# Finer waits at the down-projections, the MLP and the FFN, and the last residual adds of an out-projection ahead of a low half

## The chip, the cores and the metric

One core of one Trainium2 chip (trn2). The metric is the device time of one execution in microseconds; the number given for a kernel is the median of its runs.

## The reference

One decoder layer with pre-norms on x of shape (4, 512, 512): four batches of 512 positions with 512 features. Three sublayers follow each other, each on the layer norm of x and each added to x.

```python
x = x + _L0_attn_ref(_layernorm(x), ...)      # Mamba block, then an MLP
x = x + _L0_xattn_ref(_layernorm(x), w1, w2)  # int8 linear, silu gate, int8 linear
x = x + _L0_ffn_ref(_layernorm(x), ...)       # 4-bit weights, gelu gate
...
h = res + _mamba(_rmsnorm(hidden_states, rms1_w), ...)   # ends with y @ out_proj_w.T
hn = _rmsnorm(h, rms2_w)
mlp = silu(hn @ gate_w.T) * (hn @ up_w.T) @ down_w.T     # 2048 inner features
return h + mlp
...
inter = gelu(xt @ Wg.T) * (xt @ Wu.T)                    # 4096 inner features
out = inter @ Wd.T
```

Everything is fp32 at the interface.

## The kernel before, in words

The activations lie with features on the 128 partitions: `res` holds 4 feature tiles (f) of 4 x 512 positions. A product in nearly full fp32 is done in three passes: both operands are split into a high half (fp32r) and a low half (the rest), and `three_pass` (L1729) issues high x high (L1733), high x low (L1734) and low x high (L1735) into one PSUM bank. Weights are `ghi`/`glo`, the normed inputs of batch b are `xh[b]`/`xl[b]`, the inner activations `ahi`/`alo`. ACT makes high halves (a copy into fp32r), DVE low halves (a subtraction).

There are two phases. Phase 1 (to about 1065 us) is the Mamba scan; the change doesn't touch it. Phase 2 has these stages, written as one instruction stream per engine, tied by semaphores; nothing but the program order and the waits sets the order on an engine.

**Out-projection.** 16 chunks m, four per batch (c = m % 4), each 2 of 8 inner tiles. DVE multiplies y by silu(z) (`gate_u`, L1437), ACT makes the high half, DVE the low half (`u_low`, L1442), PE does 24 matmuls into banks 0 to 3, one per feature tile f (`out_project`, L1852). After the last chunk of a batch, `add_out` (L1448) adds the four banks to `res`, one DVE add each (L1452); it counts `outp_added`. Beside it the RMS norm of batches 0 and 1 is done: squares on ACT (L985), sums on POOL (L1217, L1220), a mean matmul (L1868), root on ACT, `rms_scale` on DVE (L1468, 4 instructions), high half on ACT (L992, counts `r_hi`), low half on DVE by `split_low` (L1475, one instruction over 128x2048, writes `xl`, counts `r_lo`). In DVE's loop over m (L1478) `split_low` of batch 0 stands at m = 13 and of batch 1 at m = 17; `add_out` of batches 1 to 3 stands at m = 9, 13 and 17, behind `rms_scale` and `split_low` of the same m. POOL adds the layer's input to `res` (`add_input`, L1209).

**MLP and FFN.** PE's loop over blocks p (L2004) has 24 groups E of 24 blocks i. The groups go through MLP half h = 0 (E 0 to 3, batches 0 and 1), MLP h = 1 (E 4 to 7, batches 2 and 3), FFN h = 0 (E 8 to 15) and FFN h = 1 (E 16 to 23). A group makes 4 inner tiles j for its two batches and projects them down:

- i = 0 to 15: gate and up products in turn, 12 matmuls each. n = i // 2 numbers the 8 pairs: tile j = n // 2, batch n % 2. Block 0 and 1 so read the first batch of the half, block 2 and 3 the second.
- ACT applies silu or gelu to the gate bank (L1094), DVE multiplies by the up bank (L1677, counts `prod_done`), ACT makes `ahi` (L1099), DVE `alo` (L1684, counts `a_lo`, in the order n = 0, 1, ... 7).
- i = 16 to 23: the down-projection, four blocks (f = 0 to 3) for the first batch, four for the second, 12 matmuls each: three per inner tile j. DVE adds each bank to `res` (`add_down`, L1663).

Blocks take banks in turn, p % 5; `bank_taken` (L1992) waits until the bank's last reader is through. Weights come by DMA into two tiles; FFN weights are unpacked on DVE (L1506 to L1510), scaled on POOL (L1231), then split (L965 on ACT, L1459 on DVE) into a ring of 5; PE waits for `w_lo`.

The waits that the change is about, at L2007 to L2010 and L2027: at the first group of each half PE waits for both batches' `xl`; block 0 waits for all 16 out-projection adds; and the first block of each batch's down-projection waits for the `alo` of that batch's last tile:

```python
if i == 0 and q == 0:
    pe.wait_ge(n_lo if ffn else r_lo, 2 * h + 2)
if p == 0:
    pe.wait_ge(outp_added, FT * B)
...
if f == 0:
    pe.wait_ge(a_lo, 8 * E + 7 + bb)
```

The second sublayer ("attention" in the code) and the norm of the third run as background steps between the blocks (`background`, L415): transposes and products on PE, and on DVE, ACT and POOL reductions, clips, scalings and norm steps, each placed at a fixed block number in each engine's loop. The norm steps' low half is again `split_low`, with `n_hi` and `n_lo`.

Of the kernel before, what the change touches and what calls it, by code (L numbers as in the profile page):

```python
# [24 lines left out]
P = 128  # L25
B, S, D = 4, 512, 512
T = B * S
FT = D // P
# [18 lines left out]
OCH = 4  # L47
# [9 lines left out]
WRING = 5  # L57
# [5 lines left out]
def build(nc, t, out):  # L63
# [79 lines left out]
    def post(name, shape, dt, at):  # L143
        return place(name, shape, dt, at)

    R1 = FREE0
    ghi = [post(f"ghi{s}", [P, 1024], F32R, R1 + 8192 * s) for s in range(WRING)]
    glo = [post(f"glo{s}", [P, 1024], F32R, R1 + 8192 * s + 4096) for s in range(WRING)]
    ahi = [post(f"ahi{j}", [P, 2 * S], F32R, R1 + 40960 + 8192 * j) for j in range(4)]
    alo = [post(f"alo{j}", [P, 2 * S], F32R, R1 + 40960 + 8192 * j + 4096) for j in range(4)]  # L150
# [61 lines left out]
    with ctx:  # L212
        def sem(name):
            return ctx.enter_context(nc.semaphore(name))
# [83 lines left out]
        outp_added = sem("outp_added")  # L298
# [7 lines left out]
        r_lo = sem("r_lo")  # L306
# [14 lines left out]
        a_lo = sem("a_lo")  # L321
        down_ready = sem("down_ready")
# [10 lines left out]
        n_lo = sem("n_lo")  # L333
# [12 lines left out]
        def cols(b, n=S):  # L346
            return slice(b * n, (b + 1) * n)
# [44 lines left out]
        def stage(Q):  # L392

            if Q < MLP_Q:
                return False, Q // MLP_PAIRS, Q % MLP_PAIRS
            return True, (Q - MLP_Q) // FFN_PAIRS, (Q - MLP_Q) % FFN_PAIRS
# [11 lines left out]
        def free_bank(V):  # L408
            return V % 5
# [14 lines left out]
        def x_step(r):  # L424
            return r - 2 if r >= 5 else r - 1 if r in (1, 2, 3) else -1

        def n_step(r):
            return r - 1 if r != 4 else -1
# [845 lines left out]
        def _(dve):  # L1274
# [47 lines left out]
            def w_low(n):  # L1322
                dve.wait_ge(whi_ready, n + 1)
                dve.tensor_tensor(wlo[n % 3][:, :, :], wraw[:, n % 2, :, :],
                                  whi[n % 3][:, :, :].bitcast(F32), ALU.subtract)\
                   .then_inc(wlo_ready, 1)
# [110 lines left out]
            def gate_u(m):  # L1437
                dve.wait_ge(sz_ready, m + 1)
                dve.tensor_tensor(uraw[m % CHUNKS][:, :, :], uraw[m % CHUNKS][:, :, :],
                                  zraw[m % CHUNKS][:, :, :], ALU.mult).then_inc(u_ready, 1)  # L1440

            def u_low(m):  # L1442
                dve.wait_ge(uhi_ready, m + 1)
                dve.tensor_tensor(ulo[m % CHUNKS][:, :, :], uraw[m % CHUNKS][:, :, :],
                                  uhi[m % CHUNKS][:, :, :].bitcast(F32), ALU.subtract)\
                   .then_inc(ulo_ready, 1)

            def add_out(b):  # L1448
                dve.wait_ge(res_loaded[b], 16)
                for f in range(FT):  # L1450
                    dve.wait_ge(outp_ready, FT * b + f + 1)
                    dve.tensor_tensor(res[:, f, cols(b)], res[:, f, cols(b)], ps[:, f, :], ALU.add)\  # L1452
                       .then_inc(outp_added, 1)
# [11 lines left out]
            def rms_scale(b):  # L1465
                dve.wait_ge(r_rooted, b + 1)
                for f in range(FT):
                    last = dve.scalar_tensor_tensor(  # L1468
                        out=xlr[b][:, f, :], in0=res[:, f, cols(b)], scalar=rms2[:, f:f + 1],
                        in1=rs_r[b % 2][:, :], op0=ALU.mult, op1=ALU.mult)  # L1470
                last.then_inc(r_scaled, 1)

            def split_low(b, hi_done, lo_done):
                dve.wait_ge(hi_done, b + 1)
                dve.tensor_tensor(xl[b][:, :, :], xlr[b][:, :, :], xh[b][:, :, :].bitcast(F32),  # L1475
                                  ALU.subtract).then_inc(lo_done, 1)

            for m in range(OCH * B + 2):  # L1478
                if m < OCH * B:
                    gate_u(m)  # L1480
                if 1 <= m <= OCH * B:
                    u_low(m - 1)
                if m in (5, 6, 11):
                    w_low((5, 6, 11).index(m))
                for b in range(2):
                    if m == OCH * b + 12:
                        rms_scale(b)
                    if m == OCH * b + 13:
                        split_low(b, r_hi, r_lo)
                if m % OCH == 1 and m > OCH:  # L1490
                    add_out(m // OCH - 1)

            link = linked(e["chain"])

# [171 lines left out]
            for p in range(24 * ALL_E + 1):  # L1666
                E, i = divmod(p, 24)
# [39 lines left out]
        def _(pe):  # L1707
# [21 lines left out]
            def three_pass(out_, pairs_, start=True, stop=True):  # L1729

                n = len(pairs_)
                for k, (w_h, w_l, x_h, x_l) in enumerate(pairs_):
                    pe.matmul(out_, w_h, x_h, start=(start and k == 0), stop=False)  # L1733
                    pe.matmul(out_, w_h, x_l, start=False, stop=False)  # L1734
                    last = pe.matmul(out_, w_l, x_h, start=False, stop=(stop and k == n - 1))  # L1735
                return last
# [115 lines left out]
            def out_project(m, f):  # L1852

                c = m % OCH
                w = slice(f * P, (f + 1) * P)
                s = m % CHUNKS
                return three_pass(ps[:, f, :], [(owhi[:, OCT * c + k, w], owlo[:, OCT * c + k, w],
                                                 uhi[s][:, k, :], ulo[s][:, k, :]) for k in range(OCT)],
                                  start=(c == 0), stop=(c == OCH - 1))
# [11 lines left out]
            def rms_var(b):  # L1871
                pe.wait_ge(r_summed, b + 1)
                bg_bank(b)
                mean(b, xhr[b])

            for m in range(OCH * B):
# [3 lines left out]
                for f in range(FT):  # L1880
                    if m >= OCH and m % OCH == 0:
                        pe.wait_ge(outp_added, FT * (m // OCH - 1) + f + 1)
                    last = out_project(m, f)
# [108 lines left out]
            def bank_taken(V):  # L1992

                if V >= 5:
                    E, i = divmod(V - 5, 24)
                    if i >= 16:
                        pe.wait_ge(added, 8 * E + i - 15)
                    elif i % 2:
                        pe.wait_ge(prod_done, 8 * E + i // 2 + 1)
                    else:  # L2000
                        pe.wait_ge(act_done, 8 * E + i // 2 + 1)
                return ps[:, free_bank(V), :]

            for p in range(24 * ALL_E):  # L2004
                E, i = divmod(p, 24)
                ffn, h, q = stage(2 * E)
                if i == 0 and q == 0:  # L2007
                    pe.wait_ge(n_lo if ffn else r_lo, 2 * h + 2)
                if p == 0:
                    pe.wait_ge(outp_added, FT * B)  # L2010
                if i < 16:
                    n, w = divmod(i, 2)
                    j, b = n // 2, 2 * h + n % 2
                    T = 6 * E + 2 * (n // 4) + w
                    at = P * (j % 2)
                    if n % 4 == 0:
                        pe.wait_ge(w_lo, T + 1)
                    three_pass(bank_taken(p), [
                        (ghi[T % WRING][:, 256 * f + at:256 * f + at + P],
                         glo[T % WRING][:, 256 * f + at:256 * f + at + P],  # L2020
                         xh[b][:, f, :], xl[b][:, f, :]) for f in range(FT)])\
                        .then_inc(up_ready if w else gate_ready, 1)
                else:
                    bb, f = divmod(i - 16, 4)
                    if i == 16:
                        pe.wait_ge(w_lo, 6 * E + 6)
                    if f == 0:  # L2027
                        pe.wait_ge(a_lo, 8 * E + 7 + bb)
                    d = [((6 * E + 4 + j // 2) % WRING, D * (j % 2) + P * f) for j in range(4)]
                    three_pass(bank_taken(p), [  # L2030
                        (ghi[s][:, at:at + P], glo[s][:, at:at + P],
                         ahi[j][:, cols(bb)], alo[j][:, cols(bb)]) for j, (s, at) in enumerate(d)])\
                        .then_inc(down_ready, 1)
                for b in (2, 3):
                    if p == 12 * (b - 2) + 3:
                        rms_var(b)
                for h_, r in background(p):
                    for bb in range(2):
                        attend(2 * h_ + bb, x_step(r - X_LEN * bb))
                    for bb in range(2):  # L2040
                        norm_step(2 * h_ + bb, n_step(r - 2 * X_LEN - 2 - bb))
# [79 lines left out]
```

## Time and profile before

| | |
|---|---|
| median of 3 runs | 2873.14 us (2871.67 to 2876.65) |
| profiled execution, its own time | 2876.27 us |
| its span | 2874.5 us |
| mean granted clock of the matrix engine | 0.944 |
| busy: PE, DVE, ACT, POOL | 2651.7 us (92%), 2129.6 (74%), 1152.1 (40%), 1255.9 (44%) |
| chain that ended last | PE 71%, DVE 11%, ACT 9%, issue 5% |

A profiled execution lists each instruction with its start and length. PE is the matrix engine, PEld its weight loads, DVE the vector engine, ACT the scalar engine, POOL GpSimd. PE's lengths overlap: a 512-column matmul is shown with 0.39 us, and the next one starts 0.23 us after it, so the distance between starts is what counts. In square brackets stands the idle time before an instruction and what released it; "issue" means that the profile found no releaser. Clocks are shares of the full 2.4 GHz.

### The profile page before, as it was taken

The page shows a single profiled execution, that of the slowest core. Times are in us where ns is not written, and L with a number is a line of the kernel's source. Part 1 is how long each engine was busy: PE and PEld are TensorE (multiplying, and loading weights), DVE is VectorE, ACT ScalarE, POOL GpSimd, SP SyncE. Part 2 cuts the span into 40 slices and gives each one's busy share as a digit, 9 for nine tenths or more (in the row PEclk, how much of TensorE's full clock was granted, in tenths as well). Part 3 has the DMA queues.
Part 4 walks back from the last instruction along what each step waited for, and adds up shares of the span by engine and source line. Part 5 has one row for each costly group of instructions (what it writes and reads, how often), then busy time and mean ns, then how long its engine had stood idle before and what let it go on. Part 6 is the DMA issues. An engine that isn't in the chain of part 4 may idle for free.

```text
span 2874.5 us, 32445 instructions
## 1 busy us (share of the span) xinstructions
PE 2651.7 (92%) x11096; PEld 1880.8 (65%) x11096; DVE 2129.6 (74%) x2731; ACT 1152.1 (40%) x1690; POOL 1255.9 (44%) x836
## 2 busy tenths in 40 slices
PE   7888888888899878999999999999989999999999
PEld 3443444444344326788887777887877788888887
DVE  4999999999999985543366677777767865555563
ACT  4555555555555534432244443443333322222221
POOL 2789888888889871110010023222212522222220
PEclk8998998989889769999999999999999999999999
DMA  6654654554465436221111112112111111111111
GB/s 230 209 157 121 188 157 121 157 166 129 132 183 154 133 99 231 81 76 49 52 66 59 45 37 67 44 45 67 44 37 45 44 49 48 51 45 52 50 47 66
DMA packets 152310, 275.35 MB, mean 96 GB/s; under 512 B 27345, under 2 KB 27857, under 8 KB 151633
## 3 DMA queue, kind: packets, MB, share of 16 engines
q1 hardware_dynamic: 152144, 273.27, 31.5%
q8 instruction: 88, 1.44, 0.2%
q14 instruction: 78, 0.63, 0.1%
HBM read 178.01 MB, written 61.34 MB: 83 GB/s over the span
## 4 chain that ended last, share of the span: by engine, by line
PE 71%; DVE 11%; ACT 9%; issue 5%; POOL 2%; DMA 1%; SPq 1%; DVEq 0%; POOLq 0%; ACTq 0%
PE ps L1733 19%; PE ps L1734 18%; PE ps L1735 18%; PE ps L1772 8%; DVE state L1358 6%; ACT ps L847 5%; PE ps L1784 4%; POOL read L1172 1%; DMA uraw<-y_d 1%; PE ps L1924 1%; PE ps L1868 1%; PE ps L1898 1%; DVE drive L1349 1%; DVE act_o L1677 0%; POOL xhr L1217 0%
## 5 line engine op out<-in xcount | busy, mean ns | idle before, releaser
L1172 POOL TENSOR_TENSOR read<-state,c_t 128x512 f32<-128x512 f32 x512 | 664.0, 1308 | 138.2 <-DVE state L1358 118.5
L1358 DVE TENSOR_TENSOR_SCAN state<-ps,drive 128x512 f32<-128x512 f32 x512 | 622.3, 1216 | 14.3 <-ACT ps L847 12.8
L1733 PE MATMUL ps<-xh,ghi 128*128 128x512 f32 x1536 | 609.1, 397 | 5.7 <-issue 5.7
L1231 POOL TENSOR_TENSOR wdeq<-packed,scales 128x1024 f32<-128x1024 f16 x96 | 260.2, 2711 | 798.3 <-DVE packed L1510 798.3
L1735 PE MATMUL ps<-xh,glo 128*128 128x512 f32 x1536 | 599.3, 390 | 0.0
L1734 PE MATMUL ps<-xl,ghi 128*128 128x512 f32 x1536 | 599.2, 390 | 0.0
L847 ACT ACTIVATE ps<-ps,a_exp 128x512 f32<-128x512 f32 x512 | 338.9, 662 | 473.8 <-PE ps L1772 472.5
L1772 PE MATMUL ps<-dpack,sel 128*128 128x512 f32 x512 | 260.9, 510 | 114.2 <-DVE state L1358 112.1
L1677 DVE TENSOR_TENSOR act_o<-act_o,ps 128x512 f32<-128x512 f32 x192 | 131.7, 686 | 313.4 <-PE ps L1735 298.5
L1349 DVE TENSOR_TENSOR drive<-ps,b_t 128x512 f32<-128x512 f32 x512 | 344.1, 672 | 12.7 <-PE ps L1772 11.9
L1099 ACT ACTIVATE ahi<-act_o 128x512 fp32r<-128x512 f32 x192 | 121.4, 632 | 562.6 <-DVE act_o L1677 562.6
L1733 PEld LDWEIGHTS ps<-xh,ghi 128*128 128x128 f32 x1536 | 289.4, 188 | 68.7 <-issue 9.2
L1734 PEld LDWEIGHTS ps<-xl,ghi 128*128 128x128 f32 x1536 | 289.4, 188 | 62.1 <-issue 3.1
L1735 PEld LDWEIGHTS ps<-xh,glo 128*128 128x128 f32 x1536 | 289.1, 188 | 60.7
L1733 PE MATMUL ps<-ahi,ghi 128*128 128x512 f32 x768 | 306.3, 399 | 20.2 <-issue 20.2
L1735 PE MATMUL ps<-ahi,glo 128*128 128x512 f32 x768 | 300.6, 391 | 0.0
L1734 PE MATMUL ps<-alo,ghi 128*128 128x512 f32 x768 | 300.6, 391 | 0.0
L1772 PE MATMUL ps<-vpack,sel 128*128 128x512 f32 x512 | 251.3, 491 | 28.6 <-DVE drive L1349 16.7
L1663 DVE TENSOR_TENSOR res<-res,ps 128x512 f32<-128x512 f32 x192 | 130.9, 685 | 192.6 <-PE ps L1735 190.0
L1772 PEld LDWEIGHTS ps<-dpack,sel 128*128 128x128 f32 x512 | 107.8, 211 | 244.1 <-DVE state L1358 235.3
L1772 PEld LDWEIGHTS ps<-vpack,sel 128*128 128x128 f32 x512 | 105.8, 207 | 225.2 <-DVE drive L1349 115.3
L965 ACT ACTIVATE ghi<-wdeq 128x1024 fp32r<-128x1024 f32 x96 | 100.9, 1051 | 297.7 <-POOL wdeq L1231 266.0
(204 smaller groups left out, 3775.3 us busy)
## 6 DMA issues: line engine op xcount, KB each, us to landing
whi<-w_d SPq DMA_DIRECT2D x63, 256.0 KB, 4.1
wlo<-w_d SPq DMA_DIRECT2D x63, 256.0 KB, 4.6
dpack<-dh SPq DMA_DIRECT2D x64, 128.0 KB, 3.8
dpack<-dl SPq DMA_DIRECT2D x64, 128.0 KB, 3.6
b_d<-ev SPq DMA_DIRECT2D x32, 256.0 KB
x_d<-ev SPq DMA_DIRECT2D x32, 256.0 KB, 2.6
vpack<-vh SPq DMA_DIRECT2D x64, 128.0 KB, 3.5
vpack<-vl SPq DMA_DIRECT2D x64, 128.0 KB, 2.8
```

The lines of the kernel that those rows point to most:

```text
L847: act.activation(ps[:, n % 2, :], ps[:, n % 2, :], ACT.Exp, scale=a_exp[:, col:col + 1]).then_inc(decay_ready, 1)
L1099: act.activation(ahi[n // 2][:, cols(n % 2)], act_o[n % 2][:, :], ACT.Copy)\
L1172: pool.tensor_tensor(read[:, n % RRING, :], state[:, n % SRING, :], c_t[:, g % 2, :], ALU.mult).then_inc(read_ready, 1)
L1231: pool.tensor_tensor(wdeq[:, :].rearrange("p (h n) -> p h n", h=2), codes, scale, ALU.mult).then_inc(deq, 1)
L1349: dve.tensor_tensor(drive[:, n % DRING, :], ps[:, 2 + n % 2, :], b_t[:, g % 2, :], ALU.mult).then_inc(drive_ready, 1)
L1358: dve.tensor_tensor_scan(state[:, n % SRING, :], ps[:, n % 2, :], drive[:, n % DRING, :], 0.0, ALU.mult, ALU.add)\
L1663: dve.tensor_tensor(res[:, f, cols(b)], res[:, f, cols(b)], ps[:, free_bank(24 * E + 16 + k), :], ALU.add).then_inc(added, 1)
L1677: dve.tensor_tensor(act_o[n % 2][:, :], act_o[n % 2][:, :], ps[:, free_bank(24 * E + 2 * n + 1), :], ALU.mult)\
L1733: pe.matmul(out_, w_h, x_h, start=(start and k == 0), stop=False)
L1734: pe.matmul(out_, w_h, x_l, start=False, stop=False)
L1735: last = pe.matmul(out_, w_l, x_h, start=False, stop=(stop and k == n - 1))
L1772: pe.matmul(ps[:, bank, :], sel[:, 4 * (j % 2) + m, :], pack[j // 2][:, :], start=True, stop=True).then_inc(done, 1)
```

## The change

In DVE's loop of the out-projection `add_out` moves ahead of `rms_scale` and `split_low` of the same m, which matters at m = 13 (adds of batch 2, low half of batch 0) and m = 17 (adds of batch 3, low half of batch 1). At the first group of a half, block 0 waits for the first batch's low half only, and block 2 for the second's. Blocks 0 to 3 wait for one add of batch 3 each, instead of block 0 for all. In a down-projection's first block of each batch, PE waits ahead of each inner tile j for that tile's `alo`; the matmuls and their order stay the same.

```diff
--- before.py
+++ after.py
@@ -1482,13 +1482,13 @@
                     u_low(m - 1)
                 if m in (5, 6, 11):
                     w_low((5, 6, 11).index(m))
+                if m % OCH == 1 and m > OCH:
+                    add_out(m // OCH - 1)
                 for b in range(2):
                     if m == OCH * b + 12:
                         rms_scale(b)
                     if m == OCH * b + 13:
                         split_low(b, r_hi, r_lo)
-                if m % OCH == 1 and m > OCH:
-                    add_out(m // OCH - 1)
 
             link = linked(e["chain"])
 
@@ -2004,10 +2004,10 @@
             for p in range(24 * ALL_E):
                 E, i = divmod(p, 24)
                 ffn, h, q = stage(2 * E)
-                if i == 0 and q == 0:
-                    pe.wait_ge(n_lo if ffn else r_lo, 2 * h + 2)
-                if p == 0:
-                    pe.wait_ge(outp_added, FT * B)
+                if q == 0 and i in (0, 2):
+                    pe.wait_ge(n_lo if ffn else r_lo, 2 * h + 1 + i // 2)
+                if p < FT:
+                    pe.wait_ge(outp_added, FT * (B - 1) + p + 1)
                 if i < 16:
                     n, w = divmod(i, 2)
                     j, b = n // 2, 2 * h + n % 2
@@ -2024,13 +2024,15 @@
                     bb, f = divmod(i - 16, 4)
                     if i == 16:
                         pe.wait_ge(w_lo, 6 * E + 6)
-                    if f == 0:
-                        pe.wait_ge(a_lo, 8 * E + 7 + bb)
-                    d = [((6 * E + 4 + j // 2) % WRING, D * (j % 2) + P * f) for j in range(4)]
-                    three_pass(bank_taken(p), [
-                        (ghi[s][:, at:at + P], glo[s][:, at:at + P],
-                         ahi[j][:, cols(bb)], alo[j][:, cols(bb)]) for j, (s, at) in enumerate(d)])\
-                        .then_inc(down_ready, 1)
+                    bank = bank_taken(p)
+                    for j in range(4):
+                        s, at = (6 * E + 4 + j // 2) % WRING, D * (j % 2) + P * f
+                        if f == 0:
+                            pe.wait_ge(a_lo, 8 * E + 2 * j + bb + 1)
+                        last = three_pass(bank, [(ghi[s][:, at:at + P], glo[s][:, at:at + P],
+                                                  ahi[j][:, cols(bb)], alo[j][:, cols(bb)])],
+                                          start=(j == 0), stop=(j == 3))
+                    last.then_inc(down_ready, 1)
                 for b in (2, 3):
                     if p == 12 * (b - 2) + 3:
                         rms_var(b)
```

## Rows read from the trace of the kernel before

**Rows 1.** windows: length, busy PE PEld DVE ACT POOL, granted clock, DMA share, GB/s

```profile
1183.00:2874.00 1691.00, 1657.99 (x7492) 1353.29 (x7492) 1062.24 (x1491) 547.97 (x744) 343.29 (x133) 0.99 0.16 51
```

**Rows 2.** waits of PE from 1176 us on: total us, times, longest

```profile
PE ps L1733 <- issue: 25.9, 7, 7.8
```

**Rows 3.** PE groups by form from 1183 us on: busy, mean ns, idle before

```profile
L1733 PE MATMUL ps<-xh,ghi 128*128 128x512 f32 x1536 | 609.1, 397 | 5.7 <-issue 5.7
...
L1733 PE MATMUL ps<-ahi,ghi 128*128 128x512 f32 x768 | 306.3, 399 | 20.2 <-issue 20.2
```

**Rows 4.** PE timeline: start us, length us, instruction, idle before

```profile
1160.74 0.39 PE L1733 MATMUL ps<-uhi,owhi 128*128 128x512 f32 x1
...
1176.84 0.39 PE L1735 MATMUL ps<-uhi,owlo 128*128 128x512 f32 x1
1182.88 0.77 PE L1733 MATMUL ps<-xh,ghi 128*128 128x512 f32 x1 [5.66 <-issue]
...
1186.22 0.40 PE L1735 MATMUL ps<-xh,glo 128*128 128x512 f32 x1
```

**Rows 5.** DVE timeline, end of the out-projection

```profile
1149.49 2.28 DVE L1475 TENSOR_TENSOR xl<-xlr,xh 128x2048 fp32r<-128x2048 f32 x1
...
1155.50 0.69 DVE L1452 TENSOR_TENSOR res<-res,ps 128x512 f32<-128x512 f32 x1 [0.68 <-PE ps L1735]
...
1157.24 1.22 DVE L1444 TENSOR_TENSOR ulo<-uraw,uhi 128x1024 fp32r<-128x1024 f32 x1
...
1170.83 2.73 DVE L1468 SCALAR_TENSOR_TENSOR xlr<-res,rms,rs_r 128x512 f32<-128x512 f32 x4
1175.54 4.85 DVE L1475 TENSOR_TENSOR xl<-xlr,xh 128x2048 fp32r<-128x2048 f32 x1 [1.99 <-ACT xh L992]
1180.31 2.47 DVE L1452 TENSOR_TENSOR res<-res,ps 128x512 f32<-128x512 f32 x4
```

**Rows 6.** PE timeline, first matmuls of six down-projections

```profile
1739.17 0.77 PE L1733 MATMUL ps<-ahi,ghi 128*128 128x512 f32 x1 [6.16 <-issue]
...
1954.84 0.47 PE L1733 MATMUL ps<-ahi,ghi 128*128 128x512 f32 x1 [2.41 <-issue]
...
2026.52 0.47 PE L1733 MATMUL ps<-ahi,ghi 128*128 128x512 f32 x1 [0.51 <-issue]
...
2104.44 0.77 PE L1733 MATMUL ps<-ahi,ghi 128*128 128x512 f32 x1 [7.78 <-issue]
...
2182.57 0.67 PE L1733 MATMUL ps<-ahi,ghi 128*128 128x512 f32 x1 [2.12 <-issue]
...
2186.29 0.39 PE L1733 MATMUL ps<-ahi,ghi 128*128 128x512 f32 x1
...
2257.62 0.47 PE L1733 MATMUL ps<-ahi,ghi 128*128 128x512 f32 x1 [1.23 <-issue]
```

**Rows 7.** DVE timeline ahead of the matmul at 2104.44

```profile
2089.82 0.68 DVE L1684 TENSOR_TENSOR alo<-act_o,ahi 128x512 fp32r<-128x512 f32 x1
...
2103.66 0.68 DVE L1684 TENSOR_TENSOR alo<-act_o,ahi 128x512 fp32r<-128x512 f32 x1
```

**Rows 8.** POOL timeline, same stretch

```profile
1173.63 4.61 POOL L1209 TENSOR_TENSOR res<-res,xraw 128x2048 f32<-128x2048 f32 x1 [3.81 <-DVE xlr L1468]
1179.31 3.29 POOL L1217 TENSOR_TENSOR xhr<-xhr 128x1024 f32<-128x1024 f32 x1 [1.07 <-ACT xhr L985]
```

**Rows 9.** windows, columns as in rows 1, after two of those waits

```profile
1954.00:1958.00 4.00, 3.17 (x18) 2.50 (x19) 3.36 (x7) 1.58 (x2) 0.00 (x0) 1.00 0.42 125
2182.00:2187.00 5.00, 4.43 (x13) 3.52 (x14) 2.96 (x5) 3.54 (x6) 0.00 (x0) 0.66 0.32 102
```

**Rows 10.** waits of DVE from 1183 us on

```profile
DVE act_o L1677 <- PE ps L1735: 298.5, 144, 5.1
```

**Rows 11.** PEld and PE timelines at a block's start

```profile
1729.91 0.19 PEld L1733 LDWEIGHTS ps<-xh,ghi 128*128 128x128 f32 x1
...
1730.13 0.39 PE L1733 MATMUL ps<-xh,ghi 128*128 128x512 f32 x1
```

## The prediction

> **What bounds the kernel now.** I read the windows first. From 1183 us to the end the matrix engine (PE) is busy 1658 of 1691 us, DVE 1062 [rows 1]. So the MLP and FFN go at PE's pace, and only what stands between its matmuls can be won. Of PE's waits from 1176 us on, one row is large: 25.9 us in 7 waits, put down to "issue", that is, to nothing the profile names [rows 2]. Grouped by form, 5.7 us of it stands before the first gate/up matmul and 20.2 us before matmuls that read ahi, the down-projections [rows 3]. The pace is 24 matmuls per 5.44 us: 71 steps from 1160.74 to 1176.84 give 0.2268 us each [rows 4].
>
> The first wait: out-projection's last matmul starts at 1176.84, the MLP's first at 1182.88 [rows 4]. What released it is on DVE: rms scale of batch 1 ends at 1173.6, xl of batch 1 (split_low) runs 1175.54 to 1180.39, the four last residual adds 1180.31 to 1182.78 [rows 5], 0.1 us before PE starts. The wait at block 0 asks for all of that, although block 0 reads batch 0 and bank 0 only.
>
> The six others stand before the first matmul of a down-projection [rows 6]; the other 18 have none. The largest ends at 2104.44; DVE ended the alo of its fourth intermediate tile at 2104.34, that of its third at 2090.50 [rows 7]. The wait is for a_lo; PE had the first three tiles' inputs 6 us before it stopped.
>
> **Part 1, start of the MLP.** Block 0 now asks for r_lo 1 (batch 0, whose split started at 1149.49 [rows 5]) and outp_added 13. The adds of batch 3 move ahead of split_low(1). Four adds cost 0.62 us each (2.47 for 4); the first three can go while PE works on the next bank, the fourth when PE is through at about 1177.2. The out-projection's chunk 15 takes 5.44 us from 1171.6, so bank 0 is full at about 1173.2, and DVE is free of rms_scale at 1173.6 [rows 5]. So add 13 is done near 1174.3 and block 0 follows the out-projection without a gap. Gained are the 6.04 us between starts less one step of 0.23: 5.81 us.
>
> Also the slow clock. After that wait 8 steps (1182.88 to 1186.22) take 3.34 us instead of 8 x 0.2268 = 1.81 [rows 4]: 1.53 us more. Without the wait this goes.
>
> What is late next: split_low(1), read by block 2 at 1177.07 + 24 x 0.2268 = 1182.5. DVE reaches it at 1178.0. With POOL at rest such a split takes 2.28 us (1149.49); beside POOL's add of 1173.63 to 1178.24 it took 4.85, ending 2.15 after POOL [rows 5, 8]. So the likely end is about 1180.4, as now: cost 0. If instead POOL's pair sum (now at 1179.31, two operations, some 4.5 us [rows 8]) goes first, the split ends near 1186.2, block 2 waits 3.7 us, and the clock penalty of 1.5 comes back: 5.2 us less. I keep that as an end. Behind split_low(1) DVE holds one weight low part and the first product; the product waits for block 1 (1182.5) in any case.
>
> The same move at m = 13 puts add_out(2) ahead of split_low(0). The adds don't move (the last one waited for PE, 1155.50), but gate_u(14) and u_low(13) come a split later, 2.28 us: u_low(13), 1157.24 now, ends near 1160.7 [rows 5]. PE's chunk 13 starts at 1160.74 [rows 4]. That is even; I take 0, at worst 0.2 us. Nothing waits for split_low(0) before 1177. No DMA is moved: SP and POOL issue the same in the same order. Sum of part 1: 5.81 + 1.53 = 7.3 us.
>
> **Part 2, down-projections.** At the first of each batch's four blocks PE now runs tiles 0 to 2, 9 matmuls or 9 x 0.2268 = 2.04 us, before it asks for the last. A gap between starts exceeds a step by the idle time + 0.16 (0.39 - 0.23). The waits [rows 6] are 6.32, 2.57, 0.67, 7.94, 2.28 and 1.39 us that way; each gives min(wait, 2.04): 2.04 + 2.04 + 0.67 + 2.04 + 2.04 + 1.39 = 10.2 us. After the wait at 2182.57, 9 steps take 3.72 us instead of 2.04 [rows 6], clock 0.66 of full, that is part of the stretch at 1.2 GHz; after the equally long one at 1954.84 it is 1.00 [rows 9]. With 0.2 us left of the wait I expect no drop: 1.7 us. After 6.32 and 7.94, 4.3 and 5.9 us are left, and the drop stays. Sum of part 2: 11.9 us.
>
> Does the gain last? DVE is late at those places through background steps (attention and norm), and gets no earlier. But between them it waits for PE, 298.5 us in 144 waits at the product alone [rows 10], so it is in step again soon and everything behind shifts. Second batch: the six waits sum to the 20.2 us of [rows 3], so it waits for nothing today, 48 steps behind the first; with the change its last tile is asked for 39 + 9 = 48 steps behind the same alo: 0.
>
> **Part 3, waits added.** Six more per down-projection, 24 of them, makes 144; with the batch and bank waits 151. A satisfied wait has no row of its own. Nearest: the block at 1730.13 stands behind a bank wait; its weight load began at 1729.91, under the matmul before, and the step is the usual 0.22 [rows 11]. So 0 each; below 0 it can't be, since a wait does no work for PE. Upper bound: the wait keeps the weight load (0.19 us) from going ahead, 151 x 0.19 = 28.7 us. I take 0, since that row is a wait of the same kind on the same engine. The batch waits at the other three stage starts stand where PE doesn't wait now (all 5.7 us before gate/up matmuls are the first one's [rows 3]): 0, covered by a norm that ends before PE gets there; without that cover they could only shorten a wait.
>
> The Trainium skill, "TensorE: Matmul & The Clock Gate", section "LDWEIGHTS (loading the stationary operand)", puts a load at its columns over 1.2 GHz, which is 107 ns here. As an estimate from that page 151 exposed loads would cost 16 us, leaving 3 us of gain where the sum without them says 19.
>
> **Sum.** 7.3 + 11.9 = 19.2 us. Against the profiled execution (2876.27 us, of which 2874.5 span) that is 2857.0. It stands 3.1 above the median 2873.14, so for the median I say 2853.9.
>
> **Rivals.** (a) Start in trouble: POOL's sums take the port first, block 2 waits for split_low(1). For it: DVE's xl did take twice its time beside POOL [rows 5, 8]. 19.2 - 5.2 = 14.0, 2859.1 us. (b) What the down-projections gain comes back as waits, because DVE, not PE, sets the pace there: only part 1 stays, 7.3, 2865.8 us. For it: in these stretches DVE holds the release. Against: DVE's own waits for PE [rows 10], and the waits stand 25 blocks or more apart (2.72 us each). (c) Slower: an added wait in front of a matmul stops the weight load from running ahead. Each then costs up to 0.19 us in all 24 down-projections, 28.7 - 19.2 = 9.5 us slower, 2882.6 us. It decides from 19.2/151 = 0.127 us per wait on. Against it stands the row at 1729.91 [rows 11]. (d) More: the clock also stays up after the two long waits, 2 x 1.5 us: 2850.8 us.
>
> **How the numbers follow.** Forecast 0.62, (a) 0.12, (b) with part losses 0.14, (c) 0.03, (d) 0.05; the last 0.04 is a partial form of (c) that ends within the measurement. A change under 0.2% (5.7 us) can't be told from none. Faster takes forecast, (a), (b) and (d) nearly whole: 0.92; same 0.05; slower 0.03. The range reaches from (d) less 2 us for the spread of runs to past (a) and into (b): 2849 to 2864, leaving out most of (b) and all of (c).
>
> **What would show it.** Right: no wait between out-projection and MLP, the adds ahead of xl on DVE, idle before matmuls that read ahi down from 20.2 to near 10 and shown before the fourth tile's matmul, two waits left over 4 us, clock near 1.00 around the fifth. Wrong: a wait at block 2, steps above 0.23 between tiles in every down-projection, or new waits in the blocks behind.

## The result, and the profile after

| | before | changed |
|---|---|---|
| median | 2873.05 us (6 runs) | 2854.12 us (6 runs, 2853.22 to 2858.70) |
| ratio, with its 95% interval | | 0.9936 (0.9924 to 0.9948) |
| profiled execution, and its span | 2876.27, 2874.5 us | 2856.02, 2854.2 us |
| mean granted clock | 0.944 | 0.943 |

The change makes the kernel 18.9 us faster. The forecast was 2853.9 us, 19.2 us less, in a range of 2849 to 2864.

PE's waits from 1170 us on, as in [rows 2] (total us, times, longest):

```profile
PE ps L1733 <- DVE alo L1684: 10.1, 3, 5.7
PE ps L1908 <- ACT x_q L1025: 3.4, 3, 2.5
PE ps L1898 <- ACT x_t L1013: 1.5, 2, 1.3
```

The row of 25.9 us put down to "issue" is gone. What is left of it is 10.1 us, and now the profile names its releaser, `alo`. The wait now stands directly before the matmul that it holds. Grouped by form, as in [rows 3], from 1173 us on so that the MLP's first matmul is in it (busy, mean ns, idle before):

```profile
L1733 PE MATMUL ps<-xh,ghi 128*128 128x512 f32 x1536 | 608.3, 396 | 0.0
...
L1733 PE MATMUL ps<-ahi,ghi 128*128 128x512 f32 x768 | 306.1, 399 | 10.2 <-DVE alo L1684 10.1
```

No idle time is left before the gate and up products (5.7 us before), and 10.2 of 20.2 us before the down-projections. The end of the out-projection on PE, as in [rows 4]:

```profile
1172.87 0.39 PE L1735 MATMUL ps<-uhi,owlo 128*128 128x512 f32 x1
1173.09 0.39 PE L1733 MATMUL ps<-xh,ghi 128*128 128x512 f32 x1
...
1178.53 0.39 PE L1733 MATMUL ps<-xh,ghi 128*128 128x512 f32 x1
```

The MLP's first matmul starts 0.22 us after the out-projection's last, where it was 6.04, and block 2, which reads batch 1, follows at 1178.53 without a wait, 24 steps of 0.227 us later. DVE in the same stretch, as in [rows 5]:

```profile
1151.40 0.69 DVE L1452 TENSOR_TENSOR res<-res,ps 128x512 f32<-128x512 f32 x1 [0.68 <-PE ps L1735]
1152.01 2.29 DVE L1475 TENSOR_TENSOR xl<-xlr,xh 128x2048 fp32r<-128x2048 f32 x1
...
1155.35 1.22 DVE L1444 TENSOR_TENSOR ulo<-uraw,uhi 128x1024 fp32r<-128x1024 f32 x1
...
1166.51 2.73 DVE L1468 SCALAR_TENSOR_TENSOR xlr<-res,rms,rs_r 128x512 f32<-128x512 f32 x4
1169.28 0.69 DVE L1452 TENSOR_TENSOR res<-res,ps 128x512 f32<-128x512 f32 x1
...
1173.29 0.69 DVE L1452 TENSOR_TENSOR res<-res,ps 128x512 f32<-128x512 f32 x1 [0.67 <-PE ps L1735]
1173.90 2.29 DVE L1475 TENSOR_TENSOR xl<-xlr,xh 128x2048 fp32r<-128x2048 f32 x1
```

The four adds of batch 3 now run from 1169.28 to 1173.98, each on its bank as PE leaves it, and `xl` of batch 1 ends at 1176.19, 2.3 us before block 2 asks for it. It takes 2.29 us, not 4.85: POOL, as in [rows 8], is through with its add at 1173.96, 0.06 us after `xl` began, and begins its pair sum only at 1175.35, after a wait for ACT.

```profile
1169.32 4.64 POOL L1209 TENSOR_TENSOR res<-res,xraw 128x2048 f32<-128x2048 f32 x1 [3.81 <-DVE xlr L1468]
1175.35 3.09 POOL L1217 TENSOR_TENSOR xhr<-xhr 128x1024 f32<-128x1024 f32 x1 [1.39 <-ACT xhr L985]
```

At m = 13 the same move puts `ulo` 3.3 us behind the last add, where it was 1.1 (1155.35 and 1152.09, the end of the add of 1151.40; rows of DVE above). That `ulo` ends at 1156.57. PE starts the chunk that reads it at 1156.64 and shows no idle time there; one step is 0.32 us instead of 0.23, 0.1 us more.

The six places of [rows 6], in the order of time. For the fourth, 2080.59 is the first matmul of its down-projection, ahead of the wait, 2088.49 the first behind it, and the lines after it are what follows up to the next transposes:

```profile
1728.03 0.76 PE L1733 MATMUL ps<-ahi,ghi 128*128 128x512 f32 x1 [4.07 <-DVE alo L1684]
...
1941.77 0.50 PE L1733 MATMUL ps<-ahi,ghi 128*128 128x512 f32 x1 [0.36 <-DVE alo L1684]
...
2010.72 0.39 PE L1733 MATMUL ps<-ahi,ghi 128*128 128x512 f32 x1
...
2080.59 0.39 PE L1733 MATMUL ps<-ahi,ghi 128*128 128x512 f32 x1
...
2088.49 0.79 PE L1733 MATMUL ps<-ahi,ghi 128*128 128x512 f32 x1 [5.70 <-DVE alo L1684]
...
2089.94 1.08 PE L1908 MATMUL ps<-ident,wqbf 128*128 128x128 bf16 x8
2091.61 1.03 PE L1908 MATMUL ps<-ident,wqbf 128*128 128x128 bf16 x8 [0.60 <-ACT x_q L1025]
2092.41 0.77 PE L1733 MATMUL ps<-ahi,ghi 128*128 128x512 f32 x1
...
2096.39 0.56 PE L1733 MATMUL ps<-ahi,ghi 128*128 128x512 f32 x1
...
2165.13 0.39 PE L1733 MATMUL ps<-ahi,ghi 128*128 128x512 f32 x1
...
2167.36 0.50 PE L1733 MATMUL ps<-ahi,ghi 128*128 128x512 f32 x1
...
2237.45 0.39 PE L1733 MATMUL ps<-ahi,ghi 128*128 128x512 f32 x1
```

The third, fifth and sixth place have no wait at their start any more. The second keeps 0.36 us, the first and the fourth 4.07 and 5.70, each after 9 matmuls. The clock around the fifth place (columns as in rows 1) is 1.00, where it was 0.66 in [rows 9]:

```profile
2164.00:2169.00 5.00, 4.97 (x22) 3.82 (x21) 4.90 (x11) 1.06 (x2) 1.71 (x1) 1.00 0.32 82
```

PE's starts can be lined up between kernels, since the blocks are the same. The table gives the length of each stretch from the out-projection's last matmul to the kernel's last, cut at the first gate or down matmul that follows a place (for the kernel before at 1229.27, 1683.17, 1762.52, 1979.65, 2048.40, 2133.85, 2208.03 and 2281.21 us), and what the change took from it:

| stretch | before | changed | gained | forecast |
|---|---|---|---|---|
| start of the MLP | 52.43 | 45.07 | 7.36 | 7.34 |
| to 1683 | 453.90 | 454.13 | -0.23 | 0 |
| first place | 79.35 | 77.41 | 1.94 | 2.04 |
| second | 217.13 | 215.05 | 2.08 | 2.04 |
| third | 68.75 | 67.95 | 0.80 | 0.67 |
| fourth | 85.45 | 86.20 | -0.75 | 2.04 |
| fifth | 74.18 | 70.55 | 3.63 | 3.72 |
| sixth | 73.18 | 71.73 | 1.45 | 1.39 |
| rest | 587.30 | 587.29 | 0.01 | 0 |
| sum | 1691.67 | 1675.38 | 16.29 | 19.24 |

So the places give 16.3 us, 3.0 less than forecast, and nearly all of the difference stands at the fourth. The column "before" is one execution of that kernel; a second one, in the experiments, has other lengths at three of these places. The two profiled executions differ by 20.3 us all the same, because in the changed kernel's the scan and the out-projection ended 3.97 us earlier (1176.84 and 1172.87). That stretch the change hardly touches. Its own scatter is in the experiments.

### The profile page after: what moved, and what is told of

Its sections match the earlier page's. It is cut to its first block, busy times and chain, and to the rows that moved or that the text cites. A ratio compares the mean times of both kernels' runs of the same rounds, so it can differ in the third digit from the quotient of the medians.

```text
span 2854.2 us, 32450 instructions
## 1 busy us (share of the span) xinstructions
PE 2650.3 (93%) x11096; PEld 1884.4 (66%) x11096; DVE 2129.0 (75%) x2731; ACT 1152.0 (40%) x1690; POOL 1256.3 (44%) x836
## 3 DMA queue, kind: packets, MB, share of 16 engines
q8 instruction: 88, 1.44, 0.2%
## 4 chain that ended last, share of the span: by engine, by line
PE 70%; DVE 11%; ACT 8%; issue 4%; POOL 3%; DMA 2%; SPq 1%; DVEq 0%; POOLq 0%; ACTq 0%
PE ps L1733 18%; PE ps L1734 18%; PE ps L1735 18%; PE ps L1772 8%; DVE state L1358 5%; ACT ps L847 5%; PE ps L1784 4%; POOL read L1172 2%; DMA vpack<-vl 1%; PE ps L1924 1%; DVE act_o L1677 1%; PE ps L1868 1%; DMA uraw<-y_d 1%; PE ps L1898 1%; DVE drive L1349 1%
## 5 line engine op out<-in xcount | busy, mean ns | idle before, releaser
L1358 DVE TENSOR_TENSOR_SCAN state<-ps,drive 128x512 f32<-128x512 f32 x512 | 624.8, 1220 | 13.1 <-ACT ps L847 11.5
L1349 DVE TENSOR_TENSOR drive<-ps,b_t 128x512 f32<-128x512 f32 x512 | 346.3, 676 | 11.9 <-PE ps L1772 11.4
L1733 PE MATMUL ps<-ahi,ghi 128*128 128x512 f32 x768 | 306.1, 399 | 10.2 <-DVE alo L1684 10.1
```

Source lines behind the costliest of these rows:

```text
L1349: dve.tensor_tensor(drive[:, n % DRING, :], ps[:, 2 + n % 2, :], b_t[:, g % 2, :], ALU.mult).then_inc(drive_ready, 1)
L1358: dve.tensor_tensor_scan(state[:, n % SRING, :], ps[:, n % 2, :], drive[:, n % DRING, :], 0.0, ALU.mult, ALU.add)\
```

## The experiments

All medians below stand beside runs of the kernel before on the same chip. Three groups of kernels ran on a chip each (before: 2875.24, 2873.58 and 2874.98 us). The edits are shown in short form, against the changed kernel unless said otherwise; `...` stands for what is left out. A step is the distance between the starts of two 512-column matmuls, 0.227 us as a rule; a slow step, of about 0.43 us, is one at the lower of the clock's two levels.

### The kernel before once more

No edit.

> The kernel before once more. The traces of before and after differ by 4.2 us before the out-projection begins (first matmul that reads uhi at 1071.74 and 1067.59 us), where the change does nothing. If that is chance, this profile lands somewhere else again, apart from 1071.7 by some us; if it belongs to the code, it lands within 0.5 us of 1071.7.

The out-projection's first matmul came at 1069.56 us, 2.2 us earlier than in the first profile of the same kernel. So the place of that matmul is chance. Over all 14 profiles it lies between 1067.05 and 1072.33 us, and the changed kernel's two profiles (1067.59, 1067.93) are in that range. Nor is the time behind it fixed. PE's timeline at the start of the MLP (start, length, instruction, idle before):

```profile
1173.91 0.39 PE L1735 MATMUL ps<-uhi,owlo 128*128 128x512 f32 x1
1180.25 0.76 PE L1733 MATMUL ps<-xh,ghi 128*128 128x512 f32 x1 [5.95 <-issue]
...
1185.93 0.56 PE L1734 MATMUL ps<-xl,ghi 128*128 128x512 f32 x1
```

Here 14 slow steps follow the wait (1180.25 to the one that begins at 1185.93). The first profile had 7; the eighth that the prediction counts there takes 0.23 us. From the out-projection's end to the last matmul this execution took 1695.05 us, 3.4 more than the first: 1.7 more at the start, 1.2 at the first place and 1.5 at the second, 1.0 less from 1229 to 1683 us, each time with more or fewer slow steps. At the second place the wait is that of [rows 6], 2.41 us there, yet 8 slow steps stand behind it, where the first profile has none:

```profile
1953.75 0.47 PE L1733 MATMUL ps<-ahi,ghi 128*128 128x512 f32 x1 [2.40 <-issue]
...
1957.27 0.59 PE L1733 MATMUL ps<-ahi,ghi 128*128 128x512 f32 x1
```

### Each part alone

```diff
 e1_start_only: down-projections
-    for j: if f == 0: pe.wait_ge(a_lo, 8 * E + 2 * j + bb + 1)
+    if f == 0: pe.wait_ge(a_lo, 8 * E + 7 + bb)
 e2_down_only: start of the halves, and DVE's order
-    if q == 0 and i in (0, 2): pe.wait_ge(..., 2 * h + 1 + i // 2)
-    if p < FT: pe.wait_ge(outp_added, FT * (B - 1) + p + 1)
+    if i == 0 and q == 0: pe.wait_ge(..., 2 * h + 2)
+    if p == 0: pe.wait_ge(outp_added, FT * B)
...
+    add_out(m // OCH - 1) behind rms_scale and split_low
```

> The adds moved and the waits of blocks 0 to 3 made fine, the down-projections' waits as before. My theory (PE sets the pace of MLP and FFN and the two parts add up): no idle between out-projection and MLP, no slow clock there, 7.2 us less than before, and the six waits before down-projections keep their 20.2 us. Rival (the parts overlap, the later waits grow when the start is earlier, because DVE or POOL sets the pace there): under 3 us less than before, with more than 20.2 us idle before matmuls that read ahi.

> Only the down-projections' waits per inner tile; start of the MLP as before. My theory from the two traces: 9 us less than before, idle before matmuls that read ahi near 10 us, and the fourth of the six places (2104 us in the kernel before) gives nothing or is worse by up to 1 us, because background transposes come 3 matmuls after the wait while the clock is low. Rival (that place's loss came from the earlier start of the MLP, a chance of phase): it gives 2 us here and the whole is 12 us.

Start only: 2863.77 us, ratio 0.9965 (0.9953 to 0.9978). Down only: 2862.21 us, 0.9958 (0.9946 to 0.9971). The six waits keep 20.3 us in the first, and `alo` keeps 10.1 us in the second. By stretches, against the first profile of the kernel before, the first gives 7.35 at the start and 0 at every other place (0.04, 0.06, 0.00, 0.02, -0.02, -0.02). The second gives 0.93, 2.06, 0.80, 0.34, 3.63 and 1.44 at the six places, together 9.2. So the parts don't touch each other. The rival of each run falls, and so does (b) of the prediction, that the gain comes back as waits. At the fourth place, where I expected between nothing and 1 us lost, 0.34 us are gained. The medians are 11.5 and 13.0 us below before, where I expected 7.2 and 9; that is 24.5 together, against 18.9 for both parts. It is more than the places give. The surplus of 5.6 us is not explained. It is no larger than the scatter of what comes ahead of the MLP: the out-projection's last matmul stands between 1169.66 and 1177.37 us over all 14 profiles (1170.94 in the first of the two).

### Is the move needed, are the waits needed

```diff
 e5_adds_behind: the change, but in DVE's loop
-    add_out(m // OCH - 1) ahead of rms_scale and split_low
+    add_out(m // OCH - 1) behind them, as before
 e6_one_wait: the change, but at the start of a half
-    if q == 0 and i in (0, 2): pe.wait_ge(..., 2 * h + 1 + i // 2)
-    if p < FT: pe.wait_ge(outp_added, FT * (B - 1) + p + 1)
+    if i == 0 and q == 0: pe.wait_ge(..., 2 * h + 2)
+    if p == 0: pe.wait_ge(outp_added, FT * B)
```

> All of the change's waits, but DVE's residual adds of batch 2 and 3 stay behind the low half. My theory: block 0 then starts on the first add, at the end of split_low, 4 us later than with the change, and the slow clock comes back: 5.5 us slower than the changed kernel, some 13.5 us faster than before. Rival (the finer waits alone do it, the move is for nothing): same as the changed kernel, 19 us faster than before.

> DVE's adds moved and down-projections fine, but block 0 waits for everything again (both low halves, all 16 adds). My theory: block 0 starts when split_low of batch 1 ends, 3 us after the out-projection's end instead of 6, the clock drops or not: 3 to 4.5 us slower than the changed kernel, 14.5 to 16 us faster than before. Rival (the move alone does it): same as the changed kernel.

Adds behind: 2860.99 us, ratio 0.9952 (0.9938 to 0.9966), 14.3 us below before. One wait: 2859.03 us, 0.9954 (0.9941 to 0.9967), 16.2 below. The MLP's first matmul in PE's timeline of the kernel with the adds behind:

```profile
1180.15 0.76 PE L1733 MATMUL ps<-xh,ghi 128*128 128x512 f32 x1 [3.35 <-DVE xl L1475]
```

DVE of the same kernel at that point:

```profile
1174.60 4.85 DVE L1475 TENSOR_TENSOR xl<-xlr,xh 128x2048 fp32r<-128x2048 f32 x1 [1.99 <-ACT xh L992]
1179.37 2.47 DVE L1452 TENSOR_TENSOR res<-res,ps 128x512 f32<-128x512 f32 x4
```

And POOL:

```profile
1172.69 4.61 POOL L1209 TENSOR_TENSOR res<-res,xraw 128x2048 f32<-128x2048 f32 x1 [3.81 <-DVE xlr L1468]
```

PE with one wait:

```profile
1179.84 0.80 PE L1733 MATMUL ps<-xh,ghi 128*128 128x512 f32 x1 [2.98 <-DVE xl L1475]
```

And DVE with one wait:

```profile
1176.89 0.69 DVE L1452 TENSOR_TENSOR res<-res,ps 128x512 f32<-128x512 f32 x1 [0.67 <-PE ps L1735]
1177.50 2.28 DVE L1475 TENSOR_TENSOR xl<-xlr,xh 128x2048 fp32r<-128x2048 f32 x1
```

With the adds behind, `xl` starts at 1174.60, 2.7 us before POOL's add is through, and takes 4.85 us, and PE waits for it and the first add, 3.35 us. With one wait, `xl` comes last and PE waits 3.0 us for it. The start stretch is 51.31 and 51.10 us, against 45.07 with the change and 52.43 before: each half of part 1 alone gains 1.1 and 1.3 us against that first profile, and without the other half some 6 of the 7.4 are lost. That is more than the 5.5 and the 3 to 4.5 I expected. The slow clock behind a wait of 3 us costs as much here as behind one of 6: counted without the wait, the start stretch is 2.7 and 2.9 us longer than the changed kernel's, each with 13 slow steps. Behind the old wait of 5.4 to 6.1 us it is 1.5 longer in the first profile of the kernel before, 2.9 in the second and 2.9 with the down-projections alone. Neither rival holds.

### What a satisfied wait costs

```diff
 e3_more_waits: gate and up blocks
-    three_pass(bank_taken(p), [... for f in range(FT)])
+    for f in range(FT):
+        pe.wait_ge(w_lo, T + 1)
+        last = three_pass(bank, [f], start=(f == 0), stop=(f == FT - 1))
```

> The changed kernel with one more satisfied wait in front of each of the 1536 groups of three matmuls in the gate and up blocks that make four per block (384 blocks), on a weight tile that is there. My theory: a satisfied wait costs nothing: within 2 us of the changed kernel, steps of 0.227 us. Rival (a wait keeps the next weight load from running ahead): 0.19 us each, up to 290 us slower; from 0.127 us each on the change itself would have lost.

2855.76 us, ratio 0.9936 (0.9922 to 0.9950), the changed kernel's own. A hundred microseconds of the MLP (length, then busy us and count of PE, PEld, DVE, ACT and POOL, granted clock, DMA share and GB/s), with the added waits:

```profile
1400.00:1500.00 100.00, 99.66 (x474) 81.48 (x473) 57.46 (x75) 43.16 (x59) 7.37 (x4) 1.00 0.17 59
```

The same stretch of the changed kernel:

```profile
1400.00:1500.00 100.00, 99.67 (x474) 81.46 (x473) 57.92 (x75) 43.62 (x59) 7.38 (x4) 1.00 0.17 58
```

Both have 474 matmuls in the 100 us. From the out-projection's end to the last matmul the kernel with 1536 more waits takes 1673.89 us, the changed one 1675.38 and, in a second profile, 1674.04. The last part of it, the "rest" of the table above, has no slow spell in any profile and is the sharper test: it holds 576 of the added waits and is 587.29 us long in both kernels. A satisfied wait costs PE nothing that can be seen, far under 1 ns each, and rival (c) of the prediction, with its 0.19 us, is out. The Trainium skill, "TensorE: Matmul & The Clock Gate", section "LDWEIGHTS (loading the stationary operand)", puts a load at its columns over 1.2 GHz, by which I estimate 107 ns for such a load; its trace length here is 0.19 us, and neither is paid for a wait.

### The fourth place

```diff
 e9_defer: PE's background steps
-    for h_, r in background(p): ...
+    for pp in () if i == 16 else (p - 1, p) if i == 17 else (p,):
+        for h_, r in background(pp): ...
```

> The changed kernel, with PE's background steps of a down-projection's first block issued behind the second block. At the fourth place the 8 transposes of wqbf (and their wait for ACT) then come 15 matmuls behind the wait, not 3. My theory (the loss there is that the slow clock lasts longer because transposes and a wait fall into it): slow steps behind that wait fall from 12 to about 7, no idle before the transposes, 2 to 3 us faster than the changed kernel. Rival (the slow spell's length is chance, as it differs by up to 1.5 us between kernels at other places): 12 slow steps or more again, within 1 us of the changed kernel.

> The changed kernel again, on this chip, as the yardstick for the other three: 2853 to 2856 us. The blocks behind 1183 us repeat to 0.1 us except where a slow-clock spell lies; the stretch before (scan and out-projection) moves by some us.

The changed kernel again came out at 2852.38 us, a little under the 2853 to 2856 I expected. 2852.81 us with the deferral, ratio 0.9921 (0.9908 to 0.9935), beside 2852.38 us, 0.9926 (0.9914 to 0.9938), for the changed kernel on the same chip: no difference that can be told. The fourth place in the trace (PE's timeline):

```profile
2093.07 0.79 PE L1733 MATMUL ps<-ahi,ghi 128*128 128x512 f32 x1 [5.69 <-DVE alo L1684]
...
2097.50 0.56 PE L1734 MATMUL ps<-alo,ghi 128*128 128x512 f32 x1
...
2098.82 1.07 PE L1908 MATMUL ps<-ident,wqbf 128*128 128x128 bf16 x16
```

The idle time before the transposes is gone, and they run at full clock behind the slow spell. But the spell has 11 slow steps, not the 7 I had from my theory. The changed kernel has 13 in both its profiles, if the step from a 512-column matmul to the transposes is counted too (my expectation says 12, without it). The stretch takes 84.15 us, against 86.20 and 86.08 in the two profiles of the changed kernel. So the deferral wins 2.0 us there: about 1.0 us by the 16 transposes (1.07 us here, 1.08 and 1.03 for each 8 at the low clock), 0.60 by the wait, and 0.4 by two slow steps less. 2 us don't show in medians whose single runs spread over 6 and 8 us.

The last term isn't the deferral's. Four other kernels have the same wait and the same transposes behind it at this place, and their spells have 7 slow steps (down only, and one wait) or 15 (adds behind, and more waits). With 7, 13 and 15 slow steps the place gives 0.34 and 0.37, -0.75 and -0.64, -1.23 and -1.19 us against the first profile of the kernel before. PE's timeline with down only, to the last slow step:

```profile
2095.76 0.79 PE L1733 MATMUL ps<-ahi,ghi 128*128 128x512 f32 x1 [5.71 <-DVE alo L1684]
...
2101.10 0.63 PE L1733 MATMUL ps<-ahi,ghi 128*128 128x512 f32 x1
```

So my theory explains 1.6 of the 2.8 us that the place fell short by, the transposes and their wait. The rival, a spell whose length is chance, is right for the rest.

### Further ahead of the wait

```diff
 e4_look1, e8_look2, e7_look3: look = 1, 2, 3 for the first batch, else 0
+    ahead = range(look + 1) if f == 0 else [f + look] if f + look < FT else []
+    if look and f: part(f, (3,)).then_inc(down_ready, 1)
+    for f_ in ahead:
+        bank_taken(p - f + f_)
+        part(f_, (0, 1, 2))
+    if not (look and f): part(f, (3,)).then_inc(down_ready, 1)
```

`part(f, js)` runs inner tiles js of feature tile f in its own bank; the waits per tile stand in it for f = 0.

> The changed kernel, and before PE waits for the fourth inner tile of the first batch it also does tiles 0 to 2 of the next feature tile, in the next bank (18 matmuls ahead of the wait instead of 9). My theory: two waits of 4.2 and 5.8 us shrink by 2.0 us each, one of 0.5 goes: 4 to 5 us faster than the changed kernel, 23 us faster than before. Rival (DVE's pace there gives it back as waits at the background steps, as at the fourth place): within 2 us of the changed kernel.

> As e4 with two feature tiles ahead: 27 matmuls, 6.1 us, before the wait. Theory: between e4 (2849) and e7 (2857), since the waits for alo it removes come back at background steps that now stand with 3 matmuls between them: 2850 to 2854 us. Rival: it is the best of the three, since it covers the whole wait of 4.2 us and most of the one of 5.8: 2844 to 2847 us.

> As e4, but tiles 0 to 2 of all four feature tiles first: 36 matmuls, 8.2 us, ahead of the wait. My theory: no wait for alo is left (10.2 us), the clock stays up (4 us): up to 14 us faster than the changed kernel, less what background steps, which now come with 3 matmuls between them, wait for; I expect 6 to 12 us. Rival: background steps eat it all, same or slower than e4.

> e4 and e9 together. Theory: their gains add, 5 + 2.5 us, so 2846 to 2848 us. Rival: with 18 matmuls ahead of the wait the deferral has nothing left to win: as e4, 2849 us.

| kernel | median | ratio (95% interval) | out-projection's end to last matmul |
|---|---|---|---|
| changed, twice | 2854.12, 2852.38 | 0.9936, 0.9926 | 1675.38, 1674.04 |
| look 1 | 2849.32 | 0.9915 (0.9901 to 0.9929) | 1666.15 |
| look 2 | 2847.71 | 0.9904 (0.9891 to 0.9918) | 1665.21 |
| look 3 | 2857.50 | 0.9942 (0.9930 to 0.9955) | 1675.99 |
| look 1 and deferral | 2846.33 | 0.9904 (0.9891 to 0.9918) | 1667.20 |

`look` is the number of feature tiles whose tiles 0 to 2 go ahead of the wait: 18, 27 or 36 matmuls instead of 9. One tile ahead behaves as expected. PE's wait for `alo`:

```profile
PE ps L1733 <- DVE alo L1684: 5.7, 2, 3.7
```

It falls from 10.1 to 5.7 us. Two ahead is better than I expected and nearly as good as its rival said: the first place gives 7.55 us there (1.94 with the change), because the wait and its slow spell are both gone. With look 1 and 2 the stretch from 1229 to 1683 us, which has no wait for `alo`, is also shorter than in the changed kernel's two profiles, by 1.6 to 2.9 us. There the clock stayed up, as it did with the added waits of the section before last, so this part isn't the edit's. The six places alone give 15.6 and 16.5 us, against 9.2 in both profiles with the change. Three ahead loses all of it again. PE's waits with look = 3:

```profile
PE ps L1908 <- DVE wqbf L1532: 5.6, 3, 3.1
PE ps L1908 <- ACT x_q L1025: 4.4, 3, 2.5
PE ps L1898 <- DVE x_a L1557: 3.6, 1, 3.6
PE ps L1898 <- ACT x_t L1013: 3.4, 2, 3.1
PE ps L1868 <- POOL xhr L1220: 1.4, 2, 1.1
```

None is for `alo`. The time came back before the background's transposes: 5.6 us for `wqbf`, 3.6 for `x_a`, 3.4 for ACT's transposed tiles, more idle than in the changed kernel (0.6, 0, 1.5). The slow spells are three, as in the changed kernel, and shorter together (14 us, against 21 and 17 in its two profiles). But at the fifth place, where the changed kernel has no slow spell, 7 slow steps now stand behind the wait for `wqbf`. In a down-projection three blocks now have 3 matmuls each between two background steps; that this is too few for DVE and ACT to finish theirs is how I read these waits. I had expected 6 to 12 us gained, and the rival was right.

The last kernel is the fastest measured, 2846.33 us, 6.1 us below the changed kernel on the same chip and 28.7 below before; look 2 at 2847.71 can't be told from it. By its trace the deferral adds 2.15 us at the fourth place (3.25 instead of 1.10), and 3.2 us were lost elsewhere in that execution: 1.6 at the first place, where look 1 has no slow spell and this one 8 slow steps, and 1.6 from 1229 to 1683 us. The medians, on two chips, leave it open whether the two gains add, as I expected, or not.

## Why the prediction was right

**Part 1, 7.34 us.** The start stretch gave 7.36 us in one profile and 7.35 in the other. The wait of 5.8 us held. The slow clock of 1.5 us was read from the same profile that the gain is measured against, and the second profile of the kernel before has 2.9 us there: against it the start gives 9.1 us. So the agreement to 0.02 us is luck in the choice of profile. The end of `split_low` was put at 1180.4 on the old time line, for POOL's add; it came 0.2 us earlier by its own count (1176.19, with the whole stretch 4.0 us earlier), and block 2 didn't wait. Rival (a) would have shown a wait at 1178.53; POOL's pair sum began 1.5 us after `xl`, not ahead of it. The even race at m = 13 cost 0.1 us at most, which was in its bounds.

**Part 2, 11.90 us.** Measured are 9.15 and 9.24 us. The waits did what was said at all six places: the third, fifth and sixth vanished, the others gave the 9 matmuls, and at the fifth the clock stayed up. Against the first profile of the kernel before, five places of six come out within 0.13 us. That closeness is partly luck at the first and second. At the first, the slow spell has 7 slow steps before and 8 after; other kernels with these waits have 12 or 13 there and gain about 1 us. Against the second profile of the kernel before, the six places give 11.9 us, since its first and second are longer.

The term that failed is the fourth place: "9 matmuls, 2.04 us" was right for the wait (5.70 us are left of 7.78), but not for what follows it. The nine matmuls done early were also the ones that had stood between the wait's end and the next background step. So only 3 were left before 8 transposes, 8 more waited for ACT (0.60 us), and all 16 ran at the low clock (1.0 us more); the granted clock is 0.50 from 2087 to 2092 us. Besides, 13 slow steps are seen instead of 7 (1.2 us more), and that part is the scatter of the spell. Together that is 2.8 us: the place cost 0.75 us instead of giving 2.04. The "drop stays" of the prediction should have been priced: what follows the drop decides how much of it is paid.

**Part 3, 0.** Shown: 1536 added waits cost nothing.

**The sum.** 19.2 us was forecast, 18.9 measured between medians, 16.3 and 17.6 by place in two profiles of the changed kernel, counted from the first profile of the kernel before, and 19.7 and 21.0 counted from its second. The forecast lies between. The agreement of the medians to 0.3 us is partly luck, as slow spells and the scan scatter by some us from one execution to the next.

## What to carry to other kernels

Where an in-order engine sets the pace, a wait should ask for what the next instruction reads and stand right before it: 1536 satisfied ones cost nothing here, and independent work moves in front of it. Splitting the wait and ordering the producer go together; either alone gained 1.1 or 1.3 us here, both 7.4. What runs ahead of a wait is taken from behind it, so look at what stands there next: with 9 to 27 matmuls moved ahead the kernel gained, with 36 it lost the gain at the next steps that need other engines.

## What the runs showed that I had not expected

- The slow spell after a wait has no fixed length. After the wait at the MLP's start it was 7 slow steps in one profile of the kernel before and 14 in another, at about 0.2 us more a step. The stretch from 1229 to 1683 us, whose one wait over 1 us is 2.5 us for ACT, took 451.3 to 454.2 us in 13 profiles (look 3 has one more wait there), and in three of them the clock stayed up. Nor does a wait's length alone decide whether the clock drops: behind 2.12 us it did at 2182.57, behind 2.41 it did not at 1954.84 ([rows 6, 9]), and behind the same wait, 2.40 us, it did in the kernel's second profile.
- `xl` (DVE) is held up by POOL's add. In the nine profiles where 0.2 to 2.7 us of the add were left when it began, it ended 2.15 or 2.16 us after the add and took 2.35 to 4.86 us; in the other five, with 0.06 us left or less, it took 2.28 or 2.29. POOL's add itself took 4.61 to 4.65 us in all of them.
- Part of PE's idle time that a profile puts down to "issue" is a semaphore wait: all 20.2 us of it before the down-projections turned into `alo`'s name or vanished when the wait moved to the matmul that needs it.
